# A cross-attention kernel with its value products and softmax sums gathered into one visit per unit instead of two

## The reference

```python
# layer 0: softmax cross-attention, 16 heads of 32
Q = (x @ Wq.T + bq), K = (ctx @ Wk.T + bk), V = (ctx @ Wv.T + bv), split into heads
att = softmax(Q K^T / sqrt(32))
x1 = layernorm(att V @ Wo.T + bo + x) * gamma0 + beta0
# layer 1: linear attention with phi = elu
KV = phi(ctx)^T ctx;  Z = 1 / (phi(x1) . sum(phi(ctx)) + 1e-6)
out = layernorm(x1 + (phi(x1) KV) * Z) * gamma1 + beta1
```

## Time and profile before

| | |
|---|---|
| Time, median of 3 runs | 1592.95 us (1592.57 to 1593.81) |
| The profiled execution | 1593.17 us, of which the span is 1591.9 us |
| Mean granted TensorE clock | 0.985 of full speed |
| Busy share of the span | PE 97%, DVE 77%, POOL 69%, ACT 52% |
| DMA | 171.06 MB, 107 GB/s over the span |

### The profile page before, as it was taken

The page is one execution under the profiler, slowest core; times in us unless marked ns, Lnnn a source line. Parts: engine busy times, 40 slices in busy tenths (PEclk is TensorE's granted clock), DMA queues, the critical chain, the costliest instruction groups (busy, mean ns, idle before and its releaser), DMA issues.

```text
span 1591.9 us, 30289 instructions
## 1 busy us (share of the span) xinstructions
PE 1542.1 (97%) x10912; PEld 1037.1 (65%) x10912; DVE 1225.6 (77%) x2399; ACT 821.5 (52%) x1577; POOL 1098.2 (69%) x1012
## 2 busy tenths in 40 slices
PE   7989999999999999999999999999999999999996
PEld 5756667676766767667676676667667666766552
DVE  3767776767788787976778788886777877798887
ACT  1454554544555555655455455655455555565541
POOL 0365765657778787866678787776678878786881
PEclk9999999999999999999999999999999999999999
DMA  8634235351523426244242524425242342410000
GB/s 241 204 127 141 87 91 162 111 144 42 156 77 104 122 80 187 69 124 130 78 117 64 160 83 125 148 72 155 70 133 74 102 132 89 135 61 28 14 29 33
DMA packets 160340, 171.06 MB, mean 107 GB/s; under 512 B 21824, under 2 KB 122176, under 8 KB 160192
## 3 DMA queue, kind: packets, MB, share of 16 engines
q1 hardware_dynamic: 155968, 167.30, 34.9%
q10 hardware_dynamic: 4224, 1.84, 0.5%
HBM read 126.10 MB, written 42.99 MB: 106 GB/s over the span
## 4 chain that ended last, share of the span: by engine, by line
PE 89%; DVE 4%; DMA 2%; issue 2%; POOL 1%; ACT 1%; SPq 0%; ACTq 0%; DVEq 0%; POOLq 0%
PE score L437 15%; PE acc L469 15%; PE scoreT L451 14%; PE misc L510 7%; PE misc L522 7%; PE misc L486 7%; PE misc L538 7%; PE misc L499 7%; PE misc L546 6%; PE acc L476 3%; DVE maxes L739 1%; PE misc L530 1%; DMA bv_col<-bv_in 1%; ACT p_ring L612 1%; DMA ctx_nat<-ctx_in 0%
## 5 line engine op out<-in xcount | busy, mean ns | idle before, releaser
L969 POOL TENSOR_TENSOR pair_sum<-p_ring 128x512 f32<-128x512 f32 x512 | 664.4, 1308 | 366.4 <-DVE pair_sum L772 209.6
L612 ACT ACTIVATE p_ring<-scoreT 128x512 f32<-128x512 f32 x1024 | 602.1, 596 | 609.1 <-PE scoreT L451 603.8
L739 DVE TENSOR_REDUCE maxes<-score 128x1 f32<-128x512 f32 x1024 | 682.6, 679 | 236.8 <-PE score L437 232.2
L437 PE MATMUL score<-k_stack,q_stack 96*128 96x512 f32 x1024 | 647.0, 632 | 21.8 <-DVE maxes L739 15.6
L451 PEld LDWEIGHTS scoreT<-q_stack,k_stack 104*128 104x128 f32 x2048 | 386.5, 192 | 186.4 <-ACT p_ring L612 106.6
L451 PE MATMUL scoreT<-q_stack,k_stack 104*128 104x256 f32 x2048 | 427.1, 290 | 6.1 <-ACT p_ring L612 5.5
L437 PEld LDWEIGHTS score<-k_stack,q_stack 96*128 96x128 f32 x1024 | 194.1, 190 | 197.3 <-issue 141.6
L469 PE MATMUL acc<-p_ring,v_sb 128*32 128x256 f32 x4096 | 256.2, 392 | 0.0
L469 PEld LDWEIGHTS acc<-p_ring,v_sb 128*32 128x32 f32 x4096 | 122.3, 112 | 89.0 <-issue 9.4
L976 POOL TENSOR_TENSOR pair_sum<-pair_sum 128x512 f32<-128x512 f32 x128 | 163.9, 1281 | 0.0
L510 PE MATMUL misc<-wv,ctxT_sb 128*128 128x128 f32 x1024 | 134.8, 275 | 0.2 <-DVE k_low L812 0.2
(11 more groups left out here) (81 smaller groups left out, 1232.2 us busy)
## 6 DMA issues: line engine op xcount, KB each, us to landing
xT_sb<-xT_in SPq DMA_DIRECT2D x62, 512.0 KB, 3.7
k_stack<-k_dram SPq DMA_DIRECT2D x96, 256.0 KB, 4.2
q_stack<-q_dram SPq DMA_DIRECT2D x192, 128.0 KB, 2.5
k_dram<-k_high SPq DMA_DIRECT2D x32, 256.0 KB, 2.2
k_dram<-k_low SPq DMA_DIRECT2D x32, 256.0 KB, 2.2
q_dram<-q_high SPq DMA_DIRECT2D x64, 128.0 KB, 1.7
q_dram<-q_low SPq DMA_DIRECT2D x64, 128.0 KB, 1.9
ctx_nat<-ctx_in SPq DMA_DIRECT2D x32, 256.0 KB, 4.9
```

What stands on the lines that cost most here:

```text
L437: pe.matmul(score[k % 3][:], q_stack[0:SPLIT, unit % NQ, j, t * P:(t + 1) * P], k_stack[0:SPLIT, group_of[unit] % 2 * QUAD + j, h * HALF:( ...
L612: act.activation(p_ring[:, n % NP, h * HALF:(h + 1) * HALF], scoreT[k % 2][:], ACT.Exp, scale=SCALE).then_inc(A["exped"], 1)
L739: dve.reduce_max(maxes[:, unit % 2, t, j, h:h + 1], score[k % 3][:], AX.X).then_inc(V["maxed"], 1)
L969: pool.tensor_tensor(pair_sum[:, place_of_pair(pair), cols], p_ring[:, (n - 1) % NP, cols], p_ring[:, n % NP, cols], ALU.add).then_inc(L[" ...
```

## The change

- There is **one visit per unit**, at `LEAD` + 16, with all eight key tiles and one group of ones matmuls.
- The eight exponential tiles are summed **serially** into one `exp_sum`. POOL adds the low half for key tiles 1 to 7 (`add_low`), and the high half for 4, 5 and 6; DVE adds the high half for 1, 2, 3 and 7 (`add_high`). That is 10 POOL and 4 DVE additions per unit, where it was 10 and 2.
- The ring has **nine slots** instead of eight. An exponential that reuses a slot waits for the visit's last matmul (`divided`).
- **`split_max` has three stages.** The high parts come from a second maximum over `maxes`, written in reduced precision, in the same stage as `max_row`. The copy is gone.
- In the half step after a visit, ACT and DVE issue their layer-norm and feature work (`finishing`) ahead of the exponential and the maximum.
- The low parts of queries and keys are made one half step later on DVE, and their DMAs `put_queries` and `put_keys` go one half step later; `put_max` and `stack_max` go one earlier.
- The planner allows 50 in a visit's half step, lets a booking run over into the next half step, allows norms on DVE for **every** tile where they end earlier there, spaces the tiles by 20 half steps instead of 21, and starts O six half steps earlier behind its unit.

```diff
-    NQ, NP, NO, NX = 3, 8, 19, 3
+    NQ, NP, NO, NX = 3, 9, 19, 3
-    VISIT = 4
-    VISITS = KT * UNITS // VISIT
-    VISIT_AT = LEAD + 13
+    VISIT_AT = LEAD + UT
+    HIGH_ON_POOL = (4, 5, 6)
+    HIGH_ON_DVE = (1, 2, 3, 7)
-        pair_sum = sb("pair_sum", [P, 2, QUAD * CH])
+        exp_sum = sb("exp_sum", [P, QUAD * CH])
-        TILE_TICKS = 21
+        TILE_TICKS = 20
...
+        def span(k):
+            return 50 if visiting(k) is not None else 14
         def find(name, engine, k, cost):
-            while k in steps or room[engine].get(k, 0) + cost > (26 if visiting(k) is not None else 14):
+            while k in steps or load.get(k, 0) + cost > span(k) and (
+                    load.get(k, 0) > span(k) - 4 or
+                    load.get(k, 0) + cost + load.get(k + 1, 0) > span(k) + span(k + 1)):
...
-            if tile >= TILES - KT and ended_on_dve < find(f"shift{norm}", "POOL", scaled + 2, 13):
+            if ended_on_dve < find(f"shift{norm}", "POOL", scaled + 2, 13):
...
-            def visit(v):
-                unit, part = divmod(v, KT // VISIT)
-                for s in range(VISIT):
-                    n = VISIT * v + s
+            def visit(unit):
+                for kt in range(KT):
+                    n = KT * unit + kt
                     pe.wait_ge(A["exped"], 2 * (n + 1))
...
-                pe.wait_ge(L["quad_low"], v + 1)
-                pe.wait_ge(V["quad_high"], v + 1)
+                pe.wait_ge(L["low_added"], (KT - 1) * (unit + 1))
+                pe.wait_ge(V["high_on_dve"], len(HIGH_ON_DVE) * (unit + 1))
                 for j in range(QUAD):
                     mm = pe.matmul(acc[j * DK:(j + 1) * DK, CH:2 * CH], ones[:, 0:DK],
-                                   pair_sum[:, place_of_pair(2 * v), j * CH:(j + 1) * CH], start=False,
-                                   stop=part == KT // VISIT - 1, tile_position=(0, j * DK), skip_group_check=True)
+                                   exp_sum[:, j * CH:(j + 1) * CH], start=False, stop=True,
+                                   tile_position=(0, j * DK), skip_group_check=True)
...
                 if h == 0 and n >= NP:
-                    act.wait_ge(T["weighted"], (n - NP) // VISIT + 1)
-                    act.wait_ge(L["paired"], 2 * ((n - NP) // 2 + 1))
+                    act.wait_ge(T["divided"], (n - NP) // KT + 1)
...
+                    dve.tensor_reduce(parts[:, :, 0:QUAD], maxes[:, u], AX.X, ALU.max,
+                                      negate=True).then_inc(V["max_high"], 1)
                 elif stage == 1:
-                    dve.tensor_copy(parts[:, :, 0:QUAD], max_row[:]).then_inc(V["max_high"], 1)
...
+            def add_high(unit, kt):
+                n, cols = KT * unit + kt, slice(HALF, 2 * HALF)
+                before = exp_sum[:, cols] if kt > 1 else p_ring[:, (n - 1) % NP, cols]
+                if kt - 1 in HIGH_ON_POOL:
+                    dve.wait_ge(L["high_on_pool"], len(HIGH_ON_POOL) * (unit + 1))
+                elif kt > 1:
+                    dve.wait_ge(V["high_on_dve"], len(HIGH_ON_DVE) * unit + HIGH_ON_DVE.index(kt))
+                elif unit > 0:
+                    dve.wait_ge(T["divided"], unit)
+                dve.wait_ge(A["exped"], 2 * n + 2)
+                dve.tensor_tensor(exp_sum[:, cols], before, p_ring[:, n % NP, cols],
+                                  ALU.add).then_inc(V["high_on_dve"], 1)
...
+            def add_low(unit, kt):
+                n, cols = KT * unit + kt, slice(0, HALF)
+                before = exp_sum[:, cols] if kt > 1 else p_ring[:, (n - 1) % NP, cols]
+                if kt > 1:
+                    pool.wait_ge(L["low_added"], (KT - 1) * unit + kt - 1)
+                elif unit > 0:
+                    pool.wait_ge(T["divided"], unit)
+                pool.wait_ge(A["exped"], 2 * n + 1)
+                pool.tensor_tensor(exp_sum[:, cols], before, p_ring[:, n % NP, cols],
+                                   ALU.add).then_inc(L["low_added"], 1)
```

More of the change, by code:

```diff
@@ L207, in book @@
             when[name][k] = tile
-            take(engine, k, cost)
+            rest = max(0, room[engine].get(k, 0) + cost - span(k))
+            take(engine, k, cost - rest)
+            take(engine, k + 1, rest)
             return k
@@ L309, in follow @@
             take("ACT", end, cost[0])
-            take("DVE", end, cost[1])
+            take("DVE", end + (kind in "KQ"), cost[1])
             if kind == "Q" and i > 0:
-                put = send("put_queries", end + 1, i, 2, False)
+                put = send("put_queries", end + 2, i, 2, False)
                 if i < NQ:
@@ L357, in build @@
         for tile in range(NX):
-            fetch(tile, 100)
+            fetch(tile, 120)
         k = FIRST
@@ L685, in keep_kv, with finishing @@
                 act.activation(kv_sb[:, i % G, :], bank_of("S", i)[:], ACT.Copy).then_inc(A["kv_kept"], 1)
+            def finishing(k):
+                for norm in range(2):
+                    if k in when[f"normalise{norm}"]:
+                        normalise(when[f"normalise{norm}"][k], norm)
+                if k in when["below"]:
+                    fall(when["below"][k])
+                if k in when["grow"]:
+                    grow(when["grow"][k])
             act.dma_start(wq[:, 0], WqT[:, 0:P].rearrange("(t p) n -> p t n", p=P)).then_inc(M["wq0"], 16)
@@ L720, in scalar_program @@
                     context_features(piece)
-                for norm in range(2):
-                    if k in when[f"normalise{norm}"]:
-                        normalise(when[f"normalise{norm}"][k], norm)
-                if k in when["below"]:
-                    fall(when["below"][k])
-                if k in when["grow"]:
-                    grow(when["grow"][k])
+                if visiting(k - 1) is None:
+                    finishing(k)
         def vector_program():
@@ L766, in split_max @@
                     dve.transpose(max_turned[:, u, :], neg_max[:].bitcast(F32)).then_inc(V["max_turned"], 1)
-            def add_quad(v):
-                first, second = (pair_sum[:, place_of_pair(2 * v + i), HALF:2 * HALF] for i in range(2))
-                dve.wait_ge(L["paired"], 4 * (v + 1))
-                dve.tensor_tensor(first, first, second, ALU.add).then_inc(V["quad_high"], 1)
+            def add_high(unit, kt):
[10 more added lines that the diff above has]
+                                  ALU.add).then_inc(V["high_on_dve"], 1)
             def normalise(unit, stage):
                 if stage == 0:
-                    dve.wait_ge(T["divided"], KT // VISIT * (unit + 1))
+                    dve.wait_ge(T["divided"], unit + 1)
                     if unit > 0:
@@ L1042, in gpsimd_program @@
             for k in range(FIRST, LAST):
+                unit, i = divmod(k - LEAD - 2, UT)
+                if 0 <= unit < UNITS and i > 1 and i % 2 == 0:
+                    add_low(unit, i // 2)
+                if 0 <= unit < UNITS and i % 2 and i // 2 in HIGH_ON_POOL:
+                    add_high(unit, i // 2)
                 piece = sum_piece(k + 2)
```

164 lines of the change are left out of this document (79 added, 85 removed).

## The result

The changed kernel takes 1668.52 us in the median of 4 runs (1665.56 to 1673.25), and the kernel before beside it 1592.76 (1590.86 to 1593.81, 4 runs). The ratio is 1.048, with a 95% interval of 1.0448 to 1.0512: 4.8% slower, where 1.4% faster was forecast and 1607 was the top of the range. The profiled execution took 1671.31 us, and its mean granted clock is 0.962 instead of 0.985.

What follows compares the result with a forecast made beforehand. PE was taken to bound dense units and DVE light ones. Dense gain -41, bunching +10, light units 0, context sums +5, clock +5, tail -3 made -24 on 1593.17: 1569, stated as 1570 us, range 1545 to 1607.

Steps and rivals of the forecast that it cites:

- Work up 2, idle down 2: I take 0 for the 11 units.: Light units, few side pieces, at DVE's pace: added DVE work offset by less idle; 0, bounds -8 to +33 us.
- in bunches of 14 that is about 11 light units, and 53 dense: Count from the code: some 150 half steps without side piece, assumed bunched; the 53 dense units run at PE's pace.
- 10 for pieces that bunch: Dense units: one more open half step each; bunched, 3.5 more units become light, 16 us back; 10 taken.
- 5 for the context sums: Context-sum stretches: DVE already nearly full, another addition overruns by about 0.3 us per eight half steps; 5 us back.
- 5 for the clock: PE's clock: more stalls bring the half clock behind them; 5 us added.
- If the pieces just close up and the empty steps stay scattered, nothing is lost.: Dense units' newly opened half steps: 0 us given back if scattered, 16 us if bunched.
- PE's own steps: -49 for the vanished visits: PE: 64 visits vanish at 0.77 us each, 49 us of steps; 41 us of it seen in 53 dense units.
- The size of an addition: 1.0 forecast: DVE's additions, 128 to 256, at 1.0 us each (bounds 0.68 and 1.82): 150 us more DVE work.
- Hidden behind 3.4 us of value matmuls: Ones matmuls' wait for POOL's last low sum, about 2.6 us, covered by the visit's value matmuls at no cost.
- That rival (chance 0.09): The serial sum is late and the ones wait for it beyond 3.4 us: 51 us on 1546, 1597 us; chance 0.09.
- DVE becomes the bound: Rival: DVE additions cost 1.6 us, deciding over 1.4: 1607 us, or 1639 at the 1.82 bound; chance 0.14.
- The tail, -3: End of the kernel: the last unit's result comes five half steps earlier; 3 us off, between 0 and 6.

Runs made afterwards that it cites:

- edit 2: Changed kernel with two of DVE's four additions per unit left out (key tiles 2 and 3), planner's schedule kept: 1595.09 us, ratio 1.0006.
- edit 4: Changed kernel with value products in two runs of 16 matmuls, one ones group, and two DVE additions per unit left out: 1655.08 us, ratio 1.0378.
- 3: Changed kernel with value products in two runs of 16 matmuls and one ones group, all additions kept: 1666.85 us, ratio 1.046.
- edit 9: edit 4 with the ones group and the normalise stages two half steps later: 1624.05 us, ratio 1.0205.
- 17: Changed kernel with all additions, value products in two runs, ones and normalise stages two half steps later: 1649.70 us, ratio 1.0356.
- edit 11: Kernel before, two visits kept, with one high-half pair sum per visit moved from POOL to DVE: 1610.05 us, ratio 1.0117.
- edit 15: Changed kernel with ones matmuls reading tile 7 and tile 3's high half from the ring, norms on DVE only in the last eight tiles: 1661.96 us.
- Edit 10: Kernel before with the planner's rules, the orders of issue and the three-stage maxima: 1582.89 us, ratio 0.9942.
- edit 5: Changed kernel with DVE's additions for key tiles 2 and 3 replaced by one-input reductions at the same places: 1619.82 us, ratio 1.0171.
- edit 1: Kernel before with the three-stage maxima alone (second maximum instead of the copy): 1587.28 us, ratio 0.9966.
- edits 8 and 12: First-pass score matmuls issued twice where there is no side piece: in the changed kernel 1670.84 us, in the kernel of Edit 10 1587.88 us.
- edits 13 to 15: Changed kernel, ones matmuls reading tile 7 from the ring: 1675.09 us; also tile 3's high half: 1667.38; that with norms mostly off DVE: 1661.96.

## Why the prediction was wrong

**The step that failed** is the one for light units: "Work up 2, idle down 2: I take 0 for the 11 units." The work did go up, but DVE's idle time for scores did not go down: it rose, from 232.2 to 258.8 us. With it failed the count, "in bunches of 14 that is about 11 light units, and 53 dense", which took every other unit at PE's pace. The units can be counted in both traces, from one unit's first value matmul to the next one's, in 63 stretches. What each lasts beyond PE's own steps (7.5, 0.86 for each piece, and 5.0 for two visits or 4.2 for one):

| side pieces | before: units, us beyond the steps | after: units, us beyond the steps |
|---|---|---|
| every open half step | 27, 1 in all | 16, 17 in all |
| 11 and more, not full | 21, 8 | 30, 70 |
| 10 and fewer | 15, 50 | 17, 97 |

PE's steps did fall by some 49 us. But the time beyond them rose from 59 to 184, where the prediction had allowed 0 for light units (33 at most), 10 for pieces that bunch, 5 for the context sums and 5 for the clock. Half of the rise is in units with 11 to 14 pieces, which it had called dense: "If the pieces just close up and the empty steps stay scattered, nothing is lost." The empty steps did stay scattered, and that is where it was lost.

**The mechanism.** A unit has two parts. In the visit PE sends no scores for 4 us (6.5 at half clock, in a few of the 64), and DVE, with at most three scores buffered, works those off, makes one addition and stops. Outside the visit DVE has 16 maxima, three additions, the splits and the normalise stages, and PE can be three half steps ahead and no more. What one engine idles in one part it can't make up in the other. With two visits of 2.5 us the three buffered maxima (3 x 0.68 = 2.0 us) cover most of each; with one of 4 us they cover half. So added DVE work should reach the end to a larger share. Four pairs, as the time's rise over the rise of DVE's busy time; the first two differ in the run alone, the third has the ones late and 36 more norms on DVE in both, the fourth takes the additions from POOL:

| | DVE busy | time | share |
|---|---|---|---|
| one run of values (edit 2 to the changed kernel) | +106 | +73 | 0.69 |
| two runs, ones right behind (edit 4 to 3) | +127 | +12 | 0.09 |
| two runs, late ones (edit 9 to 17) | +115 | +26 | 0.22 |
| two visits (before to edit 11) | +60 | +17 | 0.29 |

The shares fit the mechanism; that three buffered scores are what sets the limit was not tested, since no run has another number of banks. In the second pair the ones' long waits could hide a part of the price.

**Against a plain reading of it** stands edit 15: 55 us of work taken off DVE with the norms gave 5. The planner puts norms where it has room, while additions are bound to the exponentials' half steps and to POOL's partial sums. That position and not amount decides between these two was argued here, not tested.

**Where the 76 us are.** Edit 10 (1583) holds the planner's rules, the orders and the three stages. One visit and a serial sum with two DVE additions (edit 2) stand at 1595, 12 us more, where PE's saved steps alone would have made it 49 less. Between these two PE's busy time falls by 27 us (1534.4 to 1507.5) and its idle time rises by 43 (43.9 to 87.2); no run says which part of the change brings it. The other two additions bring the 73, of which 36 are idle time of PE and 39 longer matmuls at the lower clock. For comparison, -10 + 12 + 73 = 75.

**Point by point.**
- PE's own steps: -49 for the vanished visits. Right: the full unit at 421.10 has steps of 24.6 and lasts 24.80, and in edit 2 PE's busy total is 35 us below before (1507.5 against 1542.1). In the changed kernel it did not fall (1546.9), since more of it ran at the half clock.
- The size of an addition: 1.0 forecast, 1.03 measured; DVE additions +158 against +150. Right. The bound of 1.82 was far off as a mean; one-input work at the same places was shorter (edit 5). POOL's lower sums after the first take 1.40 us where the pair sums took 1.31, so both sides pay.
- The second reduction: 0.155 us, no copy. Right, and worth 5.4 us by edit 1.
- Norms moved to DVE: 10 guessed, none moved (13 there before and after).
- Context sums, +5: a piece of what grew. The 14 units after with four or more S pieces last 39 us beyond their steps, the 15 before 8; in edit 2 it is 31, so that the two additions are not its main cause.
- "Hidden behind 3.4 us of value matmuls": mostly; 28.5 us of waits remained, 13.9 on PE's own lines. That rival (chance 0.09) was present, but it can't be more than 28.5 of the 76 us.
- The rival "DVE becomes the bound" was set to decide at over 1.4 us for an addition. The outcome was of its kind, at 1.03 us: the point at which it decides was wrong, since it compared DVE's sum with the unit's length instead of asking what DVE can do in each part of the unit.
- The clock, +5: too small. The fall to 0.962 goes with 39 us of longer matmuls between edit 2 and the changed kernel. The clock fell where PE waited, but whether it is a cost of its own is open after edits 8 and 12.
- The tail, -3: from the last of the ones (1633.9 us) to the end are 36 us, before 1552.2 to 1591.9, 39.7. Right.

**Still open:** why edit 9, with two DVE additions and two short runs, is 41 us above edit 10. The third narrow-tile group would account for 22 and the ones' waits for 20 by the rows, but no run separates them. Also open is why edits 13 to 15 stay 67 to 80 us above edit 2, with fewer additions than the changed kernel and in the last with DVE less busy than in edit 2, where PE's extra records account for 28 to 41.

## What to carry to other kernels

Where a fast engine alternates between feeding a slower one and a block of other work, count the buffers between them in time (here three scores, 2.0 us) and compare that with the block: what the block is longer is idle time for the slower engine. Whether two short blocks are cheaper than one long one depends on how much else the slower engine has to do: here two were 28 us faster with four additions per unit and late ones, even with four and the ones right behind, and 60 us slower with two additions. Judge added work on the slower engine by the part of the cycle in which it must run, not by its busy share over the span. Before calling units dense, count from the trace how many are. And when a change bundles several edits, time the small ones apart: here they are a gain of 0.6% inside a loss of 4.8%.

## What the runs showed of the hardware

How long DVE's additions get beside a busy POOL could be measured in place. The line of the additions in the changed kernel (shortest, median, longest in ns):

```profile
L795 DVE TENSOR_TENSOR exp_sum<-exp_sum,p_ring x192: 640/906/2978, 65.5 to 1629.9; 128x512 f32<-128x512 f32 x192
L795 DVE TENSOR_TENSOR exp_sum<-p_ring x64: 664/776/1767, 62.6 to 1613.2; 128x512 f32<-128x512 f32 x64
```

One took 2.98 us, more than one whole POOL addition on top of its own 0.64, which I had not expected and which my upper bound of 1.82 (the longest of before) did not hold. And the granted clock could be raised by repeated matmuls, from 0.962 to 0.978, with the time unchanged within the interval: what TensorE's half level (1.2 GHz) had cost and what the repeats cost came out even, and the two runs don't tell whether either is small.
